# The last MLP item's norm put off into the FFN stage, with the entry and the last tile of that stage reordered

## The reference, cut to what matters

```python
for _ in range(3):
    prev = slots
    q = _ln(slots) @ wq + bq
    attn = softmax(k @ q.T / scale) + EPS_ATTN; attn = attn / attn.sum(axis=1)
    slots = (attn.T @ v) @ wu + bu + prev
    h = _ln(slots) @ w1 + b1
    slots = gelu(h) @ w2 + b2 + slots
    slots = _ln(slots + x_cls)
x = x + slots
h = _layernorm(x) @ absmean(W_fc).T        # 256 -> 1024
h = layernorm(gelu(h), ln_w, ln_b)
x = x + h @ absmean(W_proj).T              # 1024 -> 256
```

## Time and profile before

| | us |
|---|---|
| median of 3 runs | 330.46 |
| the profiled execution's own time | 329.51 |
| its span in the profile | 327.6 |
| PE busy in the span | 313.2 |
| DVE busy | 278.0 |
| ACT busy | 227.8 |
| POOL busy | 216.5 |

### The profile page before, as it was taken

How to read it: one execution, slowest core, us unless ns; L and a number is a source line. 1 busy time by engine, 2 the same in 40 slices (tenths; PEclk the granted TensorE clock), 3 DMA queues, 4 the chain that set the end, 5 groups by cost and what they waited for, 6 DMA issues and landing times. The chain is left out here.

```text
span 327.6 us, 6157 instructions
## 1 busy us (share of the span) xinstructions
PE 313.2 (96%) x1758; PEld 259.5 (79%) x1758; DVE 278.0 (85%) x816; ACT 227.8 (70%) x504; POOL 216.5 (66%) x417
## 2 busy tenths in 40 slices
PE   8899999999999989999999889899998889999985
PEld 8788887888888878888888777688875657777764
DVE  3699976989899899998998999988797998888763
ACT  2378985967576968776768675677556868777771
POOL 3169967245679867557798564677989688856331
PEclk9999999999999999999999999999999999999999
DMA  7999000000000000000000000000000000000001
GB/s 280 327 296 395 23 1 0 0 2 0 1 3 0 1 3 0 2 1 1 0 2 0 1 2 1 1 3 0 2 0 0 2 34 34 33 32 28 7 34 64
DMA packets 5312, 13.24 MB, mean 40 GB/s; under 512 B 672, under 2 KB 672, under 8 KB 4896
## 3 DMA queue, kind: packets, MB, share of 16 engines
q1 hardware_dynamic: 4160, 10.88, 9.2%
q10 hardware_dynamic: 1120, 1.98, 1.6%
HBM read 10.76 MB, written 2.10 MB: 39 GB/s over the span
## 5 line engine op out<-in xcount | busy, mean ns | idle before, releaser
L288 DVE BATCH_NORM_STATS2 stats<-S 128x6 f32<-128x256 f32 x112 | 42.1, 416 | 9.0 <-DMA S<-ctx 3.6
L339 PE MATMUL ps_mid<-XT,KT 128*128 128x256 f32 x192 | 46.0, 383 | 3.4 <-ACT XT L355 3.4
L339 PE MATMUL ps_low<-V,PR 128*128 128x257 f32 x192 | 46.1, 382 | 0.9 <-DVE PR L886 0.6
L339 PE MATMUL ps_mid<-XT,wt 128*128 128x256 f32 x192 | 45.6, 380 | 0.8 <-ACT XT L355 0.7
L339 PE MATMUL ps_low<-wn,GT 128*128 128x256 f32 x192 | 45.4, 379 | 0.0
L339 PEld LDWEIGHTS ps_low<-V,PR 128*128 128x128 f32 x192 | 36.1, 190 | 7.4 <-DVE PR L886 2.5
L339 PEld LDWEIGHTS ps_mid<-XT,KT 128*128 128x128 f32 x192 | 34.6, 190 | 8.5 <-ACT XT L355 4.8
L306 POOL TENSOR_TENSOR lnm_ab<-lnm_mv,mhalf 128x2 f32<-128x2 f32 x24 | 17.3, 720 | 35.7 <-DVE lnm_mv L296 35.7
L339 PEld LDWEIGHTS ps_low<-wn,GT 128*128 128x128 f32 x192 | 36.3, 190 | 5.0
L339 PEld LDWEIGHTS ps_mid<-XT,wt 128*128 128x128 f32 x192 | 34.7, 190 | 5.1 <-ACT XT L355 1.2
L355 ACT ACTIVATE XT<-ps_t 128x512 f32<-128x512 f32 x56 | 33.0, 589 | 7.8 <-PE ps_t L331 7.8
(11 more groups left out here) (127 smaller groups left out, 708.0 us busy)
## 6 DMA issues: line engine op xcount, KB each, us to landing
S<-ctx SPq DMA_DIRECT2D x8, 256.0 KB, 3.8
X<-x SPq DMA_DIRECT2D x8, 256.0 KB, 3.6
out<-X SPq DMA_DIRECT2D x8, 256.0 KB, 2.0
rowv<-rows SPq DMA_DIRECT2D x1, 1920.0 KB, 10.6
wf<-w_fc_t SPq DMA_DIRECT2D x1, 1024.0 KB, 11.4
wf<-w_proj_t SPq DMA_DIRECT2D x1, 1024.0 KB, 13.6
wt<-w_tr ACTq DMA_DIRECT2D x1, 512.0 KB, 4.4
wn<-w_nat ACTq DMA_DIRECT2D x1, 512.0 KB, 5.6
```

The costliest lines, as they stand in the source:

```text
L288: dve.bn_stats(ln.st[:, at, j, 0:6], tiles[:, j]).then_inc(ln.stats_done, 1)
L339: last = pe.matmul(dst(m), lhs_t[:, c, m * P:(m + 1) * P], rhs[:, c, 0:n], start=(c == 0), stop=(c == 1))
```

## The change

The statistics of item 7's last MLP output, its scaling and its sum go into FFN tile steps 5 to 8 (DVE at the end of step 5, POOL's coefficient at the start of step 6, ACT's scaling at the end of step 7, POOL's adds at the start of step 8; item 6's two adds go from step 17 to the start of step 4). hidden_t(0) goes behind item 7's product. gelu(2) and centre(2) go ahead of square(1) and of tile step 2. result(1) goes behind the low halves of tile 2. proj waits for the two low halves one at a time. The last tile's GC is written in two pieces, and its transposes go into the pair of banks ps_low[0], which gelu(14) has left. The last item is stored as two transfers, one for each row tile. The sem counts of `x1_ready` keep their order.

```diff
+        LAST = 2 * B - 1
+        def hidden_out(r, h):
+            return ps_low[0][:, h] if r == LAST else ps_mid[h][:]
...
-            with sp.Fori(0, B) as b:
+            with sp.Fori(0, B - 1) as b:
                 sp.wait_ge(o_done, 2 * b + 2)
                 sp.dma_start(o_v[b], flat(X, b)).then_inc(stored, 16)
-            sp.wait_ge(stored, 16 * B)
+            for j in range(J2):
+                sp.wait_ge(o_done, 2 * B - 1 + j)
+                sp.dma_start(o_v[B - 1][:, j * D:(j + 1) * D],
+                             X[:, B - 1, j]).then_inc(stored, 16)
+            sp.wait_ge(stored, 16 * (B + 1))
...
+            def shifted_p(r, b):
+                pool.wait_ge(p_scaled, r * (J2 * B) + (J2 * b + J2))
+                pool.wait_ge(x_shifted, J2 * b + J2)
+                for j in range(J2):
+                    pool.tensor_tensor(X[:, b, j], X[:, b, j], XH[:, b, j], ALU.add).then_inc(x1_ready, 1)
             def ffn(b, u, rt, last=None):
                 if rt == 0:
+                    if b == 2:
+                        shifted_p(ROUNDS - 1, B - 2)
+                    if b == 3:
+                        ln_coef(pool, lnp, ROUNDS * B - 1, B - 1, shift=False)
+                    if b == 4:
+                        shifted_p(ROUNDS - 1, B - 1)
                     rstd_g(2 * b - 1, 1)
...
+                    if last and (half, b) == (1, B - 1):
+                        continue
                     ln_coef(pool, lnp if half else lnm, r * B + b, b, shift=not half)
...
+                    if half == 1 and last:
+                        if b < B - 2:
+                            shifted_p(r, b)
...
             def gelu(r, rt):
+                if r == 3:
+                    act.wait_ge(sq_done, 2)
...
             def ffn(b, u, rt, last=None):
                 r = 2 * b + rt
-                gelu(r, rt)
+                if r != 2:
+                    gelu(r, rt)
                 high_half(r - 1, 1 - rt, 0)
                 high_half(r - 1, 1 - rt, 1)
                 if r == 2:
+                    copy_high(b + 1, 1 - u)
+                square(r, rt)
+                if r != 2 and rt == 0 and (last is None or last < B - 1):
+                    copy_high(b + 1, 1 - u)
+                if r == 7:
                     scale_p(ROUNDS - 1, B - 1)
-                square(r, rt)
-                if rt == 0 and (last is None or last < B - 1):
-                    copy_high(b + 1, 1 - u)
...
                     gelu(1, 1)
+                    gelu(2, 0)
                     square(1, 1)
...
-                dve.scalar_tensor_tensor(out=GC[:, rt], in0=Gf[:, rt], scalar=gneg[:, rt:rt + 1],
-                                         in1=rowv[:, ROW_LNW:ROW_LNW + H],
-                                         op0=ALU.add, op1=ALU.mult).then_inc(gc_done, 1)
+                pieces = 2 if r == LAST else 1
+                for k in range(pieces):
+                    cut = slice(k * H // pieces, (k + 1) * H // pieces)
+                    dve.scalar_tensor_tensor(out=GC[:, rt, cut], in0=Gf[:, rt, cut], scalar=gneg[:, rt:rt + 1],
+                                             in1=rowv[:, ROW_LNW:ROW_LNW + H][:, cut],
+                                             op0=ALU.add, op1=ALU.mult).then_inc(gc_done, 1)
...
             def ffn(b, u, rt, last=None):
-                centre(r, rt)
                 if r > 2:
+                    centre(r, rt)
+                if r > 3:
                     result(b - 1, r - 2, rt)
                 low_half(r - 1, 1 - rt, 0)
                 low_half(r - 1, 1 - rt, 1)
-                if r == 2:
-                    result(0, 0, 0)
+                if r in (2, 3):
+                    result(b - 1, r - 2, rt)
+                if r == 5:
+                    mlp_moments(ROUNDS - 1, B - 1)
...
                     centre(1, 1)
+                    centre(2, 0)
...
                     if last:
                         behind_drain(s)
+                    if last and s == STEPS + 1:
+                        continue
...
             def hidden_t(r, rt):
                 pe.wait_ge(gc_done, r + 1)
+                if r == LAST:
+                    pe.wait_ge(gelu_done, r)
                 for h in range(2):
-                    if isinstance(r, int) and r == 0:
+                    if r == 0:
                         pe.wait_ge(mid_read, 2 * T_FFN + 2 * RING)
+                    elif r == LAST:
+                        pe.wait_ge(gc_done, r + h + 1)
                     else:
                         pe.wait_ge(gtl_ready, 2 * r + (h - 1))
...
             def proj(r, rt, ps=ps_t[1]):
-                pe.wait_ge(gtl_ready, 2 * r + 2)
+                pe.wait_ge(gtl_ready, 2 * r + 1)
                 if ps is ps_t[1] and not (isinstance(r, int) and r == 0):
                     pe.wait_ge(o_done, r)
                 for k in range(HT):
+                    if k == HT // 2:
+                        pe.wait_ge(gtl_ready, 2 * r + 2)
...
                 if s == STEPS:
                     rows_t(1, 1)
                     fc(0, 0, 1, 1)
+                if s == STEPS + 1:
                     hidden_t(0, 0)
```

More of the change, by code:

```diff
@@ L477, in rounds @@
                     r, half, b = it
-                    if half == 1:
+                    if half == 1 and last:
+                        if b < B - 2:
+                            shifted_p(r, b)
+                    elif half == 1:
                         pool.wait_ge(p_scaled, r * (J2 * B) + (J2 * b + J2))
[L480 to L488, removed]
+                        for j in range(J2):
+                            pool.tensor_tensor(Y[:, b, j], XH[:, b, j], row("lnp_b"), ALU.add)\
+                                .then_inc(y_ready, 1)
                 if it := item(t, s, -Q_STATS, last):
@@ L578, in high_half @@
                     act.wait_ge(o_ready, r - 1)
-                act.activation(GTh[:, rt, 4 * h:4 * h + 4].rearrange("p t k -> p (t k)"), ps_mid[h][:],
+                act.activation(GTh[:, rt, 4 * h:4 * h + 4].rearrange("p t k -> p (t k)"), hidden_out(r, h),
                                ACT.Copy).then_inc(gth_ready, 1)
@@ L809, in low_half @@
                     dve.wait_ge(o_ready, r - 1)
-                dve.tensor_tensor(GTl[:, rt, 4 * h:4 * h + 4].rearrange("p t k -> p (t k)"), ps_mid[h][:],
+                dve.tensor_tensor(GTl[:, rt, 4 * h:4 * h + 4].rearrange("p t k -> p (t k)"), hidden_out(r, h),
                                   GTh[:, rt, 4 * h:4 * h + 4].rearrange("p t k -> p (t k)"), ALU.subtract)\
@@ L819, in result, with mlp_moments @@
                                          in1=X[:, b, rt], op0=ALU.mult, op1=ALU.add).then_inc(o_done, 1)
+            def mlp_moments(r, b):
+                dve.wait_ge(low_read, 2 * ring(r, 1, b) + (2 + 2 * RING))
+                bn_rows(dve, lnp, b, S[:, b])
+                bn_sum(dve, lnp, r * B + b, b)
+                centre_gain(dve, lnp, r * B + b, b, S[:, b], XH[:, b], row("lnp_g"), p_gained)
             def ffn(b, u, rt, last=None):
@@ L893, in row_max @@
                                       ALU.max, negate=True).then_inc(max_ready, 1)
[L895 to L899, removed]
                 mid, high = item(t, s, 1, last), item(t, s, 2, last)
@@ L1093, in hidden_t @@
                     for k in range(4):
-                        last = pe.transpose(ps_mid[h][:, k * P:(k + 1) * P],
+                        last = pe.transpose(hidden_out(r, h)[:, k * P:(k + 1) * P],
                                             GC[:, rt, (4 * h + k) * P:(4 * h + k + 1) * P], ident[:])
```

## The result

The kernel after takes 326.68 us (median of 4 runs, 326.4 to 326.83), the kernel before beside it 330.38 (330.18 to 330.9): ratio 0.989, interval 0.9873 to 0.9907. That is faster, as forecast, but the gain is 3.7 us, where 328.5 (a gain of 1.95) was forecast, and the time lies under the range's low end of 326.9. The kernel after was measured twice more beside the kernel before, as after_again and after_third: 326.43 against 329.71 (ratio 0.9897, 0.9881 to 0.9912) and 326.47 against 329.6 (0.9904, 0.9889 to 0.9919). Two slow executions, one of each kernel (659.91 and 468.41 us), are left out of the first pair. So the gain is better put at 3.1 to 3.3 us.

The account below looks back on a forecast made before the run. It took PE's own chain to bound the steady FFN, with waits at the entry and last tile. Terms -2.2 + 1.3 + 0.3 - 1.0 - 0.35 = -1.95 from 329.51 gave 327.56, 328.5 on the median's scale; range 326.9 to 329.8.

Parts of the forecast that it names:

- Steps 1 and 2: FFN entry: hidden_t(0) behind item 7's product, proj(0) on its first low half; PE leads 0.88 us, fc(3) at 256.12.
- Step 3: Entry: gelu(2), centre(2) moved up, item 7's norm out; hidden_t(2) without wait, hidden_t(3) waits 0.13 + 0.15, lead 2.65 us.
- Step 4: Port in tile step 4: POOL's row shift holds GC(4) to 265.4, hidden_t(4) at 268.0; entry in all -2.2 us.
- Step 5: Item 7's norm on DVE in tile step 5: 2.02 us, of which 0.82 is free; +1.3 us (bounds 0 and 2.0).
- Step 6: POOL's moved work: item 2's row shift may hold DVE's two centring instructions; +0.3 us (bounds 0 and 1.1).
- Step 7: Last tile: hidden_t(15) follows proj(13) directly, proj(14) starts at 320.04 instead of 321.02; -1.0 us (bounds -0.6 and -1.2).
- Step 8: Last store in two: half of the 0.70 us transfer waits for the last result; -0.35 us (bounds 0 and -0.35).
- Rival B: DVE absorbs item 7's norm, which and POOL's moved work then cost 0; gain 3.55, 326.9 us; chance 0.13.
- A: Port lock at full price: centring in tile step 5 waits out a whole row shift; gain 1.2, 329.3 us; chance 0.18.
- C: ACT is the new chain at the entry, square(2) and copies hold gelu(3); gain 0.65, 329.8 us; chance 0.11.
- D: Slower: POOL late with the tile's scale, rstd_g(3) behind item 6's adds, result(3) waits; 333.7 us; chance 0.06.

Follow-up runs that it names:

- null_before: The kernel before, unchanged, measured against itself: 329.59 us, ratio 0.9997.
- before_held: The kernel before with only POOL's row shifts of items 1 to 7 ahead of apply_f and held behind a GC: 329.94 us, ratio 1.0008.
- norm_split: The kernel after with item 7's norm in two pieces, in tile steps 5 and 6, POOL's coefficient ahead of apply_f(5): 327.22 us, 0.9928 to before.
- phase_split: The kernel after with row shifts of items 1 to 7 one tile step earlier and item 7's norm in two pieces: 325.12 us, 0.9857 to before.
- shift_first: The kernel after with POOL's row shift of item 1 ahead of apply_f(3) instead of behind rstd_g(2): 326.94 us, 0.9915 to before.
- norm_absent: The kernel after without DVE's statistics and centring of item 7 in the last round: 325.77 us, 0.9881 to before.

## Why the prediction was wrong

**The time** is the first step that failed: "I make the sum against 329.51 and add 0.95 at the end". null_before and its profile, and the four later medians, show 329.5 to 329.9 as the usual time of the kernel before: the profiled execution was an ordinary one. Without the 0.95 the same sum gives 327.6, in a range of 326.0 to 328.9, which holds the result. Half of the miss of 1.8 us is this.

**The terms** are the other half: -1.95 forecast, -3.07 by the profiles.

- Steps 1 and 2: fc(2) forecast at 251.11, measured 251.18; fc(3) 256.12 and 256.25. Right.
- Step 3: hidden_t(2) was forecast at 257.85 without a wait and came at 257.98; hidden_t(3) was forecast with 0.28 of waits and had none. ACT behind gelu(1) had the order and length forecast; the low halves behind GC(3) (260.12) came at 261.33, 0.17 earlier than I had them. This was not kept: in step 4 the row shift on POOL sets the time.
- Step 4: the hold on GC(4) was as forecast. The timeline of the kernel after, with the low halves of tile 3, and below it the same low halves in the kernel before:

```profile
264.19 2.38 DVE L830 SCALAR_TENSOR_TENSOR KT<-KT,gneg,rowv 128x1024 f32<-128x1024 f32 x1
264.22 1.27 POOL L470 TENSOR_TENSOR X<-X,lnb_out 128x512 f32<-128x512 f32 x1
...
266.89 1.27 DVE L838 TENSOR_TENSOR V<-ps_mid,V 128x512 f16<-128x512 f32 x2
```

```profile
269.36 1.27 DVE L810 TENSOR_TENSOR V<-ps_mid,V 128x512 f16<-128x512 f32 x2
```

  The entry is -0.88 - 2.00 + 0.34 = -2.54, forecast -2.2, in the bounds. The 0.34 is this term's: I put the low halves 3.05 behind the start of the row shift (264.1 to 267.15), by adding up full lengths. Both traces have 2.67 (264.22 to 266.89; 266.69 to 269.36), since GC(4) ends 1.08 behind the end of the row shift and not its own 1.29, and result(2) and the low halves each start 0.07 to 0.08 before the one ahead of them ends.
- Step 5 was over-sized: +1.11 measured, 1.3 forecast. I gave DVE 0.36 of wait at result(4) and 0.46 at the low half, and nothing ahead of gneg(6). But gneg(6) at 276.00 was not tight to DVE's own work: in the kernel before it starts 0.40 behind the aggregates of item 5 (275.60), in the kernel after 0.18 (275.12 to 275.30), so 0.22 was free there; and from GC(6) to result(4) it is 1.65 before and 1.21 after, so 0.44. The 0.46, on the other hand, takes 279.14 from one view and PE's 279.60 from another, the chain. The timeline of the kernel before has hidden_t(6) earlier:

```profile
279.44 1.04 PE L1094 MATMUL ps_mid<-ident,KT 128*128 128x128 f32 x8
```

  So that slack was 0.30. With these, and 1.98 for the norm (272.26 to 274.24), the term is 1.98 - 0.22 - 0.44 - 0.30 + 0.13 = 1.15.
- Step 6 was +0.3 and is 0. This is the order on the port (timeline, kernel after):

```profile
272.26 0.74 DVE L292 BATCH_NORM_STATS2 stats<-S 128x6 f32<-128x256 f32 x2
...
273.44 0.88 DVE L327 SCALAR_TENSOR_TENSOR XH<-S,lnp_mv,rowv 128x256 f32<-128x256 f32 x2
...
273.98 1.47 POOL L470 TENSOR_TENSOR X<-X,lnb_out 128x512 f32<-128x512 f32 x1
```

  The centring came 0.54 before the row shift, and POOL paid, 0.2 us (1.47 against 1.27). The rule of the Trainium skill (SBUF — State Buffer, Who interferes with whom), that the second waits for the first to end, agrees with the trace in both orders: GC(4) took 1.10 more, and the row shift 0.2 more, where 0.3 of the centring was left. My error was in who comes first: POOL reached the row shift 0.58 later than I had it (273.98 for 273.4). On its way GC(4) had held item 6's adds (2.40 us from 265.45, for a pair that takes 1.42), and GC(5) a coefficient (1.76 us from 269.04, for one that takes 0.73).
- Not named at all: -0.29 from rows_t(5) to rows_t(7). I read the steady part as a chain of PE alone from a few of its rows; two stretches of it were 0.18 and 0.11 too long, with a GC(9) of 1.67 and a GC(11) of 1.58 us, each behind a row shift that POOL had begun 0.7 to 0.8 before, and before_held takes the excess away. GC(9) in the timeline of the kernel before:

```profile
289.48 1.27 POOL L450 TENSOR_TENSOR X<-X,lnb_out 128x512 f32<-128x512 f32 x1
...
290.17 1.67 DVE L802 SCALAR_TENSOR_TENSOR KT<-KT,gneg,rowv 128x1024 f32<-128x1024 f32 x1
```

- Step 7: -0.96 (forecast -1.0): hidden_t(15) follows proj(13) and proj(14) waits 0.34 for a low half. Step 8: -0.39 (forecast -0.35). Both right, within 0.04.

The direction came as forecast. Rival B's time, 326.9, was nearest, but not its mechanism: the norm was not absorbed. A did not come, C's ACT was not late, and D's POOL was ready: result(3) waited for PE's proj, not for its scale. D's 333.7 does not come out of its own terms (328.5 + 5.4 is 333.9, and 332.4 if the first 1.5 us are free); nothing hung on it. So the mechanism was right and its sizes off: 0.95 in the time, 0.3 in step 4, 0.2 in step 5, 0.3 in step 6, and 0.3 that no step names.

## What to carry to other kernels

Put a block of work off to where the engine that does it has slack in every step, and cut it to pieces that fit one step's slack: here DVE's 2.0 us cost PE 2.3 at the entry, 1.1 in one piece in a steady step, and 0.5 in two once the row shifts stood clear of the GCs. Where two engines hold each other up, an edit can gain or lose far from its place by phase alone: look at the long instructions of both before judging a small edit. norm_split lost 0.7 beside the row shifts as they were and gained 0.57 with them moved. Read a slack from the starts in one view, and not from lengths added up or from two views. And do not move a profiled execution's time onto another scale on the ground of three runs.

## What the runs showed of the hardware

GC on DVE (1.28 us alone) and an instruction on POOL hold each other until the first is done, in either order: GC takes 2.38 beside an add of 1.27 that starts 0.03 later by the record, and 1.83 beside two adds of 0.7, of which the second waits for it. A POOL coefficient of 0.73 takes 1.76 when GC(5) has started 0.11 before it. Of 16 GCs the kernel before has six over 1.45 us, after four, phase_split four, and in these runs tenths of a microsecond of phase decided which. What a hold costs PE differs: 1.07 us on a GC cost 0.87 in tile step 11 (shift_first), 1.10 on GC(4) cost 0.7, and 0.98 on GC(6) cost 0.35 (norm_absent). Otherwise profiles repeat closely: seven stretches of the kernel after agree within 0.06 us over three profiles.
